# First edge pass of a graph network on one core: where TensorE makes the sums of tiles 2 and 3

## The reference

```python
h = (x @ W).reshape(n, H, C)
a_src = jnp.einsum('nhc,hc->nh', h, att_src)
a_dst = jnp.einsum('nhc,hc->nh', h, att_dst)
e = a_src[src] + a_dst[dst]
e = jnp.where(e > 0, e, NEG_SLOPE * e)
m = jax.ops.segment_max(e, dst, num_segments=n)
ex = jnp.exp(e - m[dst])
denom = jax.ops.segment_sum(ex, dst, num_segments=n)
alpha = ex / denom[dst]
out = jax.ops.segment_sum(h[src] * alpha[..., None], dst, num_segments=n)
```

## Time and profile before

| what | us |
|---|---|
| median of 3 runs | 6856.87 (6795.88 to 6858.34) |
| the profiled execution, its own time | 6859.47 |
| its span, first instruction to last | 6857.5 |
| TensorE busy | 4859.2 (71%) |
| VectorE busy | 3972.7 (58%) |
| ScalarE busy | 2326.2 (34%) |
| GpSimd busy | 3357.2 (49%) |
| mean granted clock of TensorE, share of full speed | 0.813 |

### The profile page before, as it was taken

The page is one execution under the profiler, slowest core; times in us unless marked ns, Lnnn a source line. Parts: engine busy times, 40 slices in busy tenths (PEclk is TensorE's granted clock), DMA queues, the critical chain, the costliest instruction groups (busy, mean ns, idle before and its releaser), DMA issues. The chain is left out here.

```text
span 6857.5 us, 82677 instructions
## 1 busy us (share of the span) xinstructions
PE 4859.2 (71%) x21442; PEld 3529.3 (51%) x21443; DVE 3972.7 (58%) x11544; ACT 2326.2 (34%) x4547; POOL 3357.2 (49%) x3181
## 2 busy tenths in 40 slices
PE   1998687888459867779656777559985655566594
PEld 0665566666346644546435555436654444444384
DVE  9302677777856677755437777843454445444534
ACT  0333555555212233322125555433322222221132
POOL 4776666666434367740135555100007773775053
PEclk9999889888679989889557777769997777777597
DMA  2554433333344656640333222100013332333424
GB/s 45 141 139 106 120 104 103 100 102 102 78 123 133 97 169 185 182 123 1 89 85 80 73 75 72 27 16 14 14 37 101 103 101 64 100 103 77 136 68 107
DMA packets 377709, 633.66 MB, mean 92 GB/s; under 512 B 130352, under 2 KB 258451, under 8 KB 376033
## 3 DMA queue, kind: packets, MB, share of 16 engines
q0 software_dynamic: 146096, 360.51, 18.7%
q1 hardware_dynamic: 231005, 263.55, 14.7%
q10 hardware_dynamic: 308, 6.40, 0.3%
HBM read 474.19 MB, written 155.98 MB: 92 GB/s over the span
## 5 line engine op out<-in xcount | busy, mean ns | idle before, releaser
L784 POOL DMA_INDIRECT conv_rows<-rows_b,index x832 | 824.8, 991 | 1134.6 <-SPq L2707 881.7
L816 DVE TENSOR_TENSOR acc<-acc,ps 125x257 f32 (+1 forms) x1664 | 702.0, 422 | 754.4 <-PE ps L2753 580.3
L2753 PE MATMUL ps<-conv_rows,conv_weight_of 128*125 128x256 f32 x1664 | 631.9, 561 | 483.2 <-DMA conv_rows<-rows_b,index 344.3
L2753 PEld LDWEIGHTS ps<-conv_rows,conv_weight_of 128*125 128x125 f32 x1664 | 475.7, 293 | 639.4 <-issue 416.8
L784 POOL DMA_INDIRECT gat_rows<-rows,index x416 | 514.0, 1236 | 298.3 <-PE ps L1099 150.8
L333 POOL DMA_INDIRECT records_src<-by_src_edge_stage,by_src_edge_slot x400 | 430.1, 1075 | 373.9 <-issue 119.8
L784 POOL DMA_INDIRECT hyp_rows<-rows,index x416 | 417.7, 1004 | 347.9 <-PE ps L2360 213.6
L784 POOL DMA_INDIRECT mpnn_rows<-rows_b,index x416 | 456.9, 1098 | 231.7 <-issue 116.0
L2741 ACT ACTIVATE conv_weight_of<-conv_onehot_b,index 128x125 f32<-128x125 bf16 x832 | 251.5, 385 | 829.3 <-DVE conv_onehot_b L2725 829.3
L499 POOL DMA_INDIRECT records_dst<-front_back,front_dst_addr x400 | 409.6, 1024 | 218.6 <-issue 133.3
L1023 ACT CAST room<-ps 125x1024 bf16<-125x1024 f32 x416 | 404.5, 1017 | 297.6 <-PE ps L1086 290.5
(11 more groups left out here) (591 smaller groups left out, 10288.6 us busy)
## 6 DMA issues: line engine op xcount, KB each, us to landing
mpnn_edge<-records_src SPq DMA_DIRECT2D x104, 512.0 KB
edge_rows<-front_edge_ring SPq DMA_DIRECT2D x100, 451.5 KB
by_src_edge_stage<-edge_rows SPq DMA_DIRECT2D x100, 451.5 KB
conv_rows<-rows_b,index POOLq DMA_INDIRECT x832
front_attr<-in_edge_attr SPq DMA_DIRECT2D x100, 112.0 KB
rows_b<-acc SPq DMA_DIRECT2D x15, 560.0 KB
second_w<-in_L_ffn_w SPq DMA_DIRECT2D x1, 8192.0 KB
slots<-mlp_y SPq DMA_DIRECT2D x56, 128.0 KB
```

The costliest lines, as they stand in the source:

```text
L784: pool.indirect_dma_start(out=rows[:, n % U, t, :], out_offset=None, in_=table, in_offset=bass.IndirectOffsetOnAxis(ap=ends[:, n * G + t:n ...
L816: dve.tensor_tensor(here, here, S.ps[0:P, t % banks, 0:width], ALU.add).then_inc(added, 1)
L2753: pe.matmul(S.ps[0:P, t, 0:D], weight_of[:, q.slot, t, :], rows[:, q.slot, t, :], start=True, stop=True).then_inc(summed, 1)
```

## The change

The stage list of TensorE in `gat` puts all four sums 0 to 3 ahead of the look-up. Before, the sums of tiles 2 and 3 stood behind it. No instruction is added or taken away, and the waits of each stage stay as they are. The lists of the other engines are the same.

```diff
-                pipeline(pe, *spreads(0, 1, 2, 3), *sums(0, 1), (2, look_up), *sums(2, 3), (0, turn_one_hots),
+                pipeline(pe, *spreads(0, 1, 2, 3), *sums(0, 1, 2, 3), (2, look_up), (0, turn_one_hots),
                          *spreads(4, 5), *sums(4, 5), *spreads(6, 7), *sums(6, 7))
```

## The result

The changed kernel takes 6995.71 us (median of 3 runs, 6954.03 to 7003.35), the kernel before 6856.87. The ratio is 1.0197, 95% interval 1.0164 to 1.0230: slower by 2%. The forecast was 7000. The profiled execution took 7003.35 us, its span is 7001.4, which is 143.9 more than before; the working gave 143.

The account below looks back on a forecast made before the run. No engine is full; a ring of waits between TensorE and VectorE sets 20.95 us a step. The new terms sum to 23.93, 2.98 more in each of 48 steps: 143 us, so 7000 us, range 6925 to 7070.

Parts of the forecast that it names:

- The ring: Loop of waits between TensorE and VectorE that sets the step's period: 20.95 us before, forecast 23.93 with the change.
- T: Moment in each step when VectorE's tables for the look-up are ready; T to T is one step.
- T to sum 2: Tables ready to TensorE's sum of tile 2, which needs VectorE's addition of tile 0: 2.00, 0.43 and 0.06 us.
- turning to sum 6: TensorE's stretch from the turning of the one-hots to the sum of tile 6: 6.70 us, bounds 5.71 to 10.0.
- to VectorE's tile 6: From the start of TensorE's sum 6 to VectorE taking up tile 6: 0.93 us.
- to the next T: VectorE from tile 6 until the next tables are ready: 8.46 us, taken from steps of 8.56 and 8.37.
- The scores: VectorE's work behind tile 3 and the maxima: forecast near T + 9.7, behind the look-up's end at T + 7.84, without waiting.
- The first steps: Look-ups before 794, where VectorE's additions are the later side: costed at nothing, 9 us at most.
- The idle time: TensorE's idle stretch ahead of sum 2: forecast to grow from 3.28 to 5.6 us, making the slow look-up the rule.
- The weight load: Sum 2's weights on TensorE: taken to wait with the matmul; loaded early, an estimated 0.1 to 0.3 us a step less.
- The look-up's register load: TensorE's register loads behind the sums: said to issue while the sums wait, costed at nothing.
- Rival 2, the clock stays up: TensorE stays at 2.4 GHz and the change wins: 19.66 us a step, -62 us, 6795; chance 0.03.

## Why the prediction was right

**The ring and the wait.** Right, and shown twice: the wait alone, without any moved sum, takes 7010 us, and with all sums moved but the wait ended ahead of the tables the time is 6915. That isn't the 6851 of before, since the additions of tiles 0 and 1 and their register load now stand ahead of the tables on VectorE. The terms, forecast and measured in the step shown above: T to sum 2 2.49, 2.48; sums 1.92, 1.92; look-up 3.43, 3.27; turning to sum 6 6.70, 6.97; to VectorE's tile 6 0.93, 0.87; to the next T 8.46, 8.38 (1221.46 to 1229.84). Sum 23.93, 23.89. The scores, forecast at T + 9.7 behind the end of the look-up, start at T + 9.72.

**The first steps.** Costed at nothing, 9 at most; they took 10.2. The rest of the program behind the last look-up took 6.3 less, which was in no term and is within what single executions differ by. That the total came to 143.9 against 143 is in part luck: 140.0 in the steps, 10.2 more ahead of them and 6.3 less behind.

**The idle time.** Forecast 5.6, measured 4.81. The sum kept sums 0 and 1 as far ahead of T as before; TensorE is the late side now, so they end only 2.3 ahead of T (1203.6 to 1205.95), 3.1 before. The clock fell within the wait all the same, and all look-ups behind the second were slow.

**The weight load.** It waited with the sum (215.7 us), as the row of before had it. Sum 2 started at T + 2.48; nothing is seen of the 0.1 to 0.3 that the prediction estimated. The rule behind that estimate, weight loads pulled ahead of matmuls in flight, is from the Trainium skill, page "TensorE: Matmul & The Clock Gate", section "Step-by-step: what each phase is for"; in this case the load waited together with its matmul.

**The look-up's register load.** The prediction had it issue while the sums wait, and costed it at nothing. It issues behind the start of sum 2: in the step above the trace has it (TENSOR_LOAD, L847, 0.59 us) at 1209.11. Nothing was lost by that, since the sums at the low clock run until 1210.35; the term was nothing for another reason than the one given.

**Rival 2, the clock stays up.** Its price was too kind. The 9.07 us from sum 2 to sum 6 are where the change breaks even; 19.66 us a step wants 7.78 or less (19.66 - 8.46 - 0.93 - 2.49), and the prediction's own estimate of 7.9 was already above that. At the full clock TensorE needs 8.36, and the step is 20.1: the look-up starts 1.55 behind sum 2 instead of 0.94, because the second sum starts 0.58 behind the first and the register load, issued at 1277.62 and 0.59 long, is no longer covered (the 0.27 of "issue"). The gain of 1.29 a step would have been 0.85, and no filling of the idle time kept the clock up in every step.

**What was right for a reason too simple.** The forecast added fixed terms. The runs with tile 0 half a microsecond sooner and a quarter later show that the term from turning to sum 6 is not fixed: 7.44, 6.97 and 6.66 us for a start of sum 2 at T + 1.99, 2.48 and 2.75, with the same 23.9 us a step each time. That the 6.70, taken from a single slow step of before, came so close owes something to this: the step settles at 23.9 within some range of the other terms. Why the clock comes back at that point was not found out; that the step stays at 23.9 is shown for three kernels, and that it no longer does for a start at T + 3.60, on another chip, for a fourth.

## What to carry to other kernels

Before moving work into an engine's idle time, ask what that work waits for: work whose own condition is met later than what the engine was waiting for does not fill the time, it prolongs it and delays everything behind. Work that is ready then (here two tiles' spreads) does fill it, and was worth 0.6% where the change had lost 2%. Where TensorE's clock takes part in a ring, its slow stretch is no fixed price: a few tenths won or lost elsewhere may vanish in it.

## What was not expected

- Within limits the step's length did not follow its parts: 23.9 us for starts of sum 2 between T + 1.99 and T + 2.75, and 24.99 for T + 3.60 (on another chip).
- The clock fell during the look-up (1.00 to 0.84 to 0.50 within 3 us) although TensorE had idled only 0.72 and 0.30 us in the 8 us before. The long waits are one way to the low clock; the look-up's own matmuls seem to be another, which was not tested by itself.
- Taking VectorE's one-hots out from between the tables and the additions uncovered two things that they had hidden: ScalarE's factor (0.53) and, with the additions ahead of the tables, the load of the blocks' numbers into registers (0.7 to 0.8; the load itself is 0.60 long).
